# A fused attention and feed-forward kernel: value sums, output products and casts reordered, the last four steps turned by TensorE

## The chip, the cores and the metric

One core of one Trainium2 chip. The metric is the device time of the program in microseconds. Engines: PE is TensorE, DVE is VectorE, ACT is ScalarE, POOL is GpSimd, SP issues the DMAs. Each runs its own program in order and waits for the others at semaphores.

## The reference

Two layers over x of 8 x 128 x 512, each an attention and a feed-forward part with residuals. Nearly all the time goes to the attention of the first layer, with 32 heads of 128:

```python
x = _rmsnorm(hidden_states, ln_weight)
h_q = (x @ w_q.T).reshape(b, lq, H, DH)
h_k = (key_value_states @ w_k.T).reshape(b, lk, H, DH)
h_v = (key_value_states @ w_v.T).reshape(b, lk, H, DH)
score = jnp.einsum('bqhd,bkhd->bhqk', h_q, h_k) + position_bias[None]
score = jnp.where(m, score, -jnp.inf)
score = jnp.where(m, jax.nn.softmax(score, axis=-1), 0.0)
attn = jnp.einsum('bhqk,bkhd->bqhd', score, h_v).reshape(b, lq, H * DH)
return hidden_states + attn @ w_out.T
```

Then come a feed-forward part with low-rank experts, an attention of one head (its product of `wq1` and `wk1` is formed on the chip while the first attention ends), and a feed-forward part with 6-bit weights.

## The kernel before

The attention is cut into 64 steps. A group is two heads, and has four steps of two batches each, so a step holds four 128 x 128 score blocks in one PSUM bank. A turn is eight steps (c = 0 to 7, called step 0 to 7 here); turns 2 to 6 are a hardware loop, the first eight steps, turn 1 and the last turn are written out. The last four steps (60 to 63) also carry the start of the second layer.

Every fp32 operand of a large product is held as a high and a low part (`_hi` in fp32r, made by ACT as a cast; `_lo` by POOL or VectorE as a subtraction), and a product is three matmuls: high by high, high by low, low by high (`three`, lines 363 to 365). Queries and keys of a group are made by seven half-size products each (`q_p1` to `q_p7`, `k_p1` to `k_p7`), the values of two groups by seven products in two halves (`v_p1` to `v_p7`). Each product lands in a PSUM bank (`ps_q`, `ps_q2`, `ps_k`, `ps_k2`, `ps_v`), and VectorE adds it to earlier sums (`q_u2`, `k_c11`, `v_c22`, ...), which frees the bank. The seven weight combinations are formed by POOL and cast by ACT (`high_v1` to `high_v7`, `low_v`, `high_fourth`, `low_third` and so on), one step or more ahead of their use.

A step runs like this. TensorE makes the scores in `ps_s`. VectorE adds mask and bias (`softmax_front`, L1598), takes the row maximum and negates it (`neg_max`, L1602). ACT takes four exponentials with row sums (L787). VectorE forms the factors (reciprocal L1606, `row_fac` L1608) and multiplies (L1611, `softmax_back`). `turn_blocks` transposes 32 x 32 blocks twice, into `probs_t` and in place (L1616, L1617), and ACT copies the twelve off-diagonal blocks to their places (`pt_blocks`, L799). One step later TensorE multiplies by the values (`step_values`, `ps_t`, L2214); ACT casts the result to `att_hi` (`attention_high`, L781), VectorE forms `att_lo` (`attention_rest`, L1476), and TensorE multiplies by the output weights (`output`) in two halves, one batch each, into the single bank `ps_o`. VectorE adds each half into `acc` (`add_output`, L1488); half 1 cannot start until half 0 has been added.

Each engine's order is written out by hand in its own `step(i, c)`: between the parts above stand products, sums, casts and subtractions of coming groups.

## Time and profile before

| | us |
|---|---|
| median of 3 runs (1002.92 to 1004.36) | 1003.94 |
| the profiled execution | 1005.09 |
| its span, first to last instruction | 1003.1 |
| busy: TensorE 93%, VectorE 74%, ACT 60%, POOL 53% of the span | |

A timeline row has its start (from the span's start), its duration, engine, line, operation, the tile written and those read, and in brackets the idle time before it with the instruction that ended it. Matmuls overlap their neighbours, so 128x512 matmuls that take 0.39 us start about 0.23 us apart. The turn shown below starts in step 6: scores of step 7 at 557.45, of step 0 at 569.28, of step 1 at 584.28, of step 3 at 607.92.

### The profile page before, as it was taken

How to read it: one execution, taken by the hardware profiler on the slowest of the kernel's cores; microseconds unless marked ns; L12 is line 12 of the kernel's file. 1: busy time of each engine (PE TensorE's matmuls, PEld its weight loads, DVE VectorE, ACT ScalarE, POOL GpSimd, SP SyncE). 2: the span in 40 equal slices, each digit the busy share in tenths (PEclk: the TensorE clock that was granted, in tenths of full speed). 3: DMA queues.
4: the chain of work that ended last, by engine and by line, in shares of the span. 5: the costliest groups of instructions: out<-in, count | busy, mean ns of one | idle time of the engine just before them, and what ended most of it. 6: DMA issues, size and time to landing. Idle time of an engine off the chain costs nothing.

```text
span 1003.1 us, 17307 instructions
## 1 busy us (share of the span) xinstructions
PE 937.3 (93%) x5261; PEld 796.9 (79%) x5261; DVE 739.3 (74%) x1289; ACT 598.3 (60%) x1847; POOL 527.0 (53%) x582
## 2 busy tenths in 40 slices
PE   9999999999899989998999899989999897889997
PEld 8778888888788878887888778877887776768885
DVE  5676874676787787777787778777877887667787
ACT  5787556465565656665666566656574656344564
POOL 2450636365557656675457555755565643112477
PEclk9999999999999999999999999999999998899999
DMA  9214348644666457645683657364755662130101
GB/s 337 78 65 151 126 153 289 215 167 147 221 223 224 148 213 253 235 146 209 215 269 123 239 184 258 123 248 155 269 166 194 204 216 84 65 116 1 33 22 63
DMA packets 61291, 171.70 MB, mean 171 GB/s; under 512 B 6055, under 2 KB 8491, under 8 KB 60988
## 3 DMA queue, kind: packets, MB, share of 16 engines
q1 hardware_dynamic: 61244, 171.11, 49.6%
q8 instruction: 25, 0.41, 0.2%
q14 instruction: 22, 0.18, 0.1%
HBM read 159.56 MB, written 11.53 MB: 171 GB/s over the span
## 4 chain that ended last, share of the span: by engine, by line
PE 66%; DVE 14%; ACT 8%; issue 8%; POOL 3%; DVEq 1%; DMA 0%; SPq 0%; ACTq 0%; POOLq 0%
PE ps_v L363 5%; PE ps_o L363 5%; PE ps_s L2193 5%; PE ps_o L365 4%; PE ps_o L364 4%; PE ps_v L365 4%; PE ps_v L364 4%; PE ps_q L363 4%; PE ps_q L365 4%; PE ps_q L364 4%; PE ps_k L363 4%; PE ps_k L364 4%; PE ps_k L365 4%; PE ps_t L2214 3%; ACT probs_t L799 3%
## 5 line engine op out<-in xcount | busy, mean ns | idle before, releaser
L799 ACT COPY probs_t<-scores 32x128 f32<-32x128 f32 x768 | 227.6, 296 | 175.8 <-DVE scores L1617 167.6
L787 ACT ACTIVATE scores<-scores,neg_max 128x128 f32<-128x128 f32 x256 | 99.7, 391 | 110.1 <-DVE neg_max L1602 109.7
L1158 POOL TENSOR_TENSOR wq_lo<-raw_q,wq_hi 128x256 fp32r<-128x256 f32 x65 | 57.2, 881 | 150.5 <-ACT wq_hi L620 150.5
L363 PE MATMUL ps_o<-wo_hi,att_hi 128*128 128x512 f32 x256 | 106.4, 416 | 20.0 <-DVE acc L1488 16.2
L1598 DVE TENSOR_TENSOR scores<-ps_s,shift 128x512 f32<-128x512 f32 x64 | 44.2, 691 | 104.4 <-PE ps_s L2193 104.2
L364 PE MATMUL ps_o<-wo_lo,att_hi 128*128 128x512 f32 x256 | 102.4, 400 | 0.0
L365 PE MATMUL ps_o<-wo_hi,att_lo 128*128 128x512 f32 x256 | 102.4, 400 | 0.0
L1488 DVE TENSOR_TENSOR acc<-ps_o,acc 128x512 f32<-128x512 f32 x128 | 86.8, 678 | 17.2 <-PE ps_o L365 17.1
L1476 DVE TENSOR_TENSOR att_lo<-ps_t,att_hi 128x512 fp32r<-128x512 f32 x64 | 44.2, 690 | 65.6 <-ACT att_hi L781 65.6
L1117 POOL TENSOR_TENSOR shift<-bias_sb,mask_sb 128x512 f32<-128x512 f32 x64 | 87.2, 1365 | 1.5 <-DVE scores L1598 1.5
L363 PE MATMUL ps_v<-wv_hi,ct_hi 128*128 128x256 f32 x264 | 78.0, 295 | 6.3 <-DVE vv L1442 2.2
L363 PEld LDWEIGHTS ps_o<-wo_hi,att_hi 128*128 128x128 f32 x256 | 49.2, 192 | 42.7 <-DVE acc L1488 14.9
L1108 POOL TENSOR_TENSOR wo_lo<-raw_o,wo_hi 128x1024 fp32r<-128x1024 f32 x16 | 38.3, 2395 | 75.6 <-ACT wo_hi L717 75.6
L2193 PEld LDWEIGHTS ps_s<-kt,qt 128*128 128x128 f32 x512 | 67.7, 195 | 10.2 <-issue 4.3
L1611 DVE TENSOR_TENSOR scores<-scores,row_fac 128x512 f32<-128x512 f32 x64 | 73.8, 1153 | 2.2
L364 PE MATMUL ps_v<-wv_lo,ct_hi 128*128 128x256 f32 x264 | 75.3, 285 | 0.0
L365 PE MATMUL ps_v<-wv_hi,ct_lo 128*128 128x256 f32 x264 | 75.3, 285 | 0.0
L2193 PE MATMUL ps_s<-kt,qt 128*128 128x128 f32 x512 | 69.1, 278 | 2.4 <-DVE kt L1527 1.5
L363 PE MATMUL ps_v<-wv_hi,ring_hi 128*128 128x256 f32 x144 | 44.1, 306 | 19.9 <-DVE vv L1561 10.7
L363 PE MATMUL ps_q<-xt_hi,wq_hi 128*128 128x512 f32 x148 | 60.9, 411 | 0.0
L363 PEld LDWEIGHTS ps_v<-wv_hi,ct_hi 128*128 128x128 f32 x264 | 50.9, 193 | 10.7 <-issue 3.9
L365 PEld LDWEIGHTS ps_o<-wo_hi,att_lo 128*128 128x128 f32 x256 | 49.3, 193 | 11.1
(394 smaller groups left out, 2850.5 us busy)
## 6 DMA issues: line engine op xcount, KB each, us to landing
ring_hi<-scratch_x_t SPq DMA_DIRECT2D x39, 512.0 KB, 4.0
ring_lo<-scratch_x_t SPq DMA_DIRECT2D x39, 512.0 KB, 4.9
ring_hi<-scratch_c_t SPq DMA_DIRECT2D x39, 512.0 KB, 5.4
ring_lo<-scratch_c_t SPq DMA_DIRECT2D x39, 512.0 KB, 6.2
raw_o<-in_w_o SPq DMA_DIRECT2D x16, 512.0 KB, 3.3
raw_q<-in_w_q SPq DMA_DIRECT2D x15, 512.0 KB, 4.1
raw_k<-in_w_k SPq DMA_DIRECT2D x15, 512.0 KB, 5.2
xt_hi<-scratch_x_t SPq DMA_DIRECT2D x13, 512.0 KB, 5.8
```

Source lines behind the costliest of these rows:

```text
L363: pe.matmul(dst, hi_l, hi_r, start=first, stop=False)
L364: pe.matmul(dst, hi_l, lo_r, start=False, stop=False)
L365: return pe.matmul(dst, lo_l, hi_r, start=False, stop=last)
L787: e = act.activation(probs[n][:, m, :], scores[n][:, m, :], ACT.Exp, bias=neg_max[:, n, m:m + 1], accum_out=row_sum[:, n, m:m + 1])
L799: last = act.copy(block_of(probs_t, j, i), block_of(scores[n], i, j))
L1117: pool.tensor_tensor(shift[n][:].rearrange("p (b h) k -> p b h k", b=2), bias_b, mask_b, ALU.add).then_inc(shift_done, 1)
L1158: pool.tensor_tensor(w_slot(wq_lo, slot), src, w_slot(wq_hi, slot).bitcast(F32), ALU.subtract).then_inc(wq_lo_s, 1)
L1476: dve.tensor_tensor(att_lo[:], blocks(ps_t), att_hi[:].bitcast(F32), ALU.subtract).then_inc(att_lo_s, 1)
L1488: dve.tensor_tensor(acc[:, b, :], ps_o[:], acc[:, b, :], ALU.add).then_inc(o_added, 1)
L1598: dve.tensor_tensor(scores[n][:], blocks(ps_s), shift[n][:], ALU.add).then_inc(s_shifted, 1)
L1611: dve.tensor_tensor(probs[n][:], probs[n][:], row_fac[:, n, :].unsqueeze(2).broadcast_to([P, 4, P]), ALU.mult).then_inc(s_chain, 1)
L2193: last = pe.matmul(ps_s[:, m * P:(m + 1) * P], qt[n][:, h, cols], kt[n][:, h, cols], start=True, stop=True)
```

## The change

What it does, engine by engine.

- VectorE: `softmax_back` is divided. The reciprocal and `row_fac` (`row_factors`) move ahead of `attention_rest`; the multiply joins the two transposes in `turn_blocks`. In step 0 the value sums `v_c22` and `v_u4` move ahead of the multiply, in steps 1 and 2 `v_c12` moves ahead of the output sum, and the output sum of half 0 stands behind the transposes in steps 3 and 7 as in the others. In step 7 `q_c21` moves ahead of `attention_rest`, and `k_u3` behind the output sum.
- TensorE: `output` waits for `att_hi` first, issues the four matmuls that read it, and only then waits for `att_lo`. In step 4 `q_p3` goes ahead of `v_p1`.
- ACT: the value casts `high_v1`, `2`, `5`, `6`, `7` go ahead of the step's exponentials; `attention_high` goes ahead of `q_first`, and `v_first` of half 1 behind `high_sums`.
- POOL: the low value parts go ahead of the weight sums (steps 0, 4), of `low_third` (6) and of `low_fourth` (3, 7).
- The last four steps: VectorE only multiplies (`softmax_back`), TensorE transposes the four blocks into `ps_t` with `ident` (`step_transpose`), and ACT copies the bank to `probs_t` (`pt_evac`). Values are taken in the same step and no longer in the next, and the orders of all engines around them are written anew.

```diff
+WHOLE = STEPS - 4
...
+        def turned(s):
+            return not isinstance(s, int) or s < WHOLE
...
# ACT
+            def pt_evac(s):
+                act.wait_ge(pt_done, s - WHOLE + 1)
+                act.copy(probs_t[:], blocks(ps_t)).then_inc(pt_out, 1)
...
+                if c == 6 and coming:
+                    high_v7(i + 1)
...
                 exponentials(s, n)
                 if c == 4 and coming:
                     v_first(i + 1, 0)
-                    high_v2(i + 1)
+                attention_high(s - 1)
                 if c % 4 == 1 and more:
                     q_first(G)
-                attention_high(s - 1)
...
-            pt_blocks(STEPS - 4, 0, (0, 1, 2, 3))
+            pt_evac(STEPS - 4)
             wk1_high_part(3)
             split_o(GROUPS - 1)
+            attention_high(STEPS - 4)
             exponentials(STEPS - 3, 1)
-            attention_high(STEPS - 4)
...
# POOL
+                if c == 6 and coming:
+                    low_v(i + 1, 4, 0, v_even[0][:])
                 if c % 4 == 2 and more:
                     low_third(G)
...
-                if c == 6 and coming:
-                    low_v(i + 1, 4, 0, v_even[0][:])
...
# VectorE
             def softmax_front(s, n):
                 dve.wait_ge(s_done, s + 1)
                 dve.wait_ge(shift_done, s + 1)
-                wait_from(dve, e_done, s - 1)
-                wait_from(dve, pt_out, 4 * s - 4)
+                wait_from(dve, pt_out, s - 1)
...
+            for c in range(5):
                 step(TURNS - 1, c)
+            add_output(STEPS - 5, 3, (1,))
+            attention_rest(STEPS - 4)
+            softmax_front(STEPS - 3, 1)
+            q_c12(GROUPS - 1)
+            softmax_back(STEPS - 3, 1)
+            add_output(STEPS - 4, 4, (0,))
+            k_c12(GROUPS - 1)
+            wq1_rest(0)
+            wq1_rest(1)
+            add_output(STEPS - 4, 4, (1,))
+            wq1_rest(2)
...
# TensorE
             def output(s, c, g=None, parts=(0, 1)):
-                wait_from(pe, att_lo_s, s + 1)
+                wait_from(pe, att_hi_s, s + 1)
...
                     for h in range(2):
-                        last = three(pe, ps_o[:], att_hi[:, 2 * j + h, :], att_lo[:, 2 * j + h, :],
-                                     wo_hi[:, h, :], wo_lo[:, h, :], h == 0, h == 1)
+                        pe.matmul(ps_o[:], att_hi[:, 2 * j + h, :], wo_hi[:, h, :], start=h == 0, stop=False)
+                        pe.matmul(ps_o[:], att_hi[:, 2 * j + h, :], wo_lo[:, h, :], start=False, stop=False)
+                    if j == 0:
+                        wait_from(pe, att_lo_s, s + 1)
+                    for h in range(2):
+                        last = pe.matmul(ps_o[:], att_lo[:, 2 * j + h, :], wo_hi[:, h, :], start=False, stop=h == 1)
                     last.then_inc(o_done, 1)
...
+            def step_transpose(s, c):
+                pe.wait_ge(p_done, s + 1)
+                wait_from(pe, att_lo_s, s)
+                for m in range(4):
+                    last = pe.transpose(ps_t[:, m * P:(m + 1) * P], probs[c % 2][:, m, :], ident[:])
+                last.then_inc(pt_done, 1)
...
+            s = STEPS - 4
+            wait_projections(g, 4)
+            step_scores(s, 4)
+            q_p5(g)
+            step_values(s - 1, 3, v_count(TURNS - 1, 13))
+            k_p5(g)
+            v_p4(TURNS - 1, 1)
+            output(s - 1, 3, None, (0,))
+            step_transpose(s, 4)
+            output(s - 1, 3, None, (1,))
+            step_values(s, 4, v_count(TURNS - 1, 14))
+
+            s = STEPS - 3
+            wait_projections(g, 5)
+            step_scores(s, 5)
+            q_p3(g)
+            k_p3(g)
+            output(s - 1, 4, g, (0,))
...
+            step_transpose(s, 5)
+            output(s - 1, 4, None, (1,))
+            step_values(s, 5, v_count(TURNS - 1, 14))
...
             step_scores(s, 6)
             product_m(0)
-            step_values(s - 1, 5, v_count(TURNS - 1, 14))
+            output(s - 1, 5, None, (0,))
             product_m(1)
-            output(s - 1, 5, None, (0,))
+            output(s - 1, 5, None, (1,))
+            step_transpose(s, 6)
             product_m(2)
-            output(s - 1, 5, None, (1,))
+            step_values(s, 6, v_count(TURNS - 1, 14))
```

Where the instructions stand now, at three places. First VectorE in step 0 of a loop turn, from `att_lo` or the factors to the output sum. Before (`v_odd_high` and `vv` are the value sums, the first `scores` row is the multiply):

```order
L1476 TENSOR_TENSOR att_lo<-ps_t,att_hi 128x512
L1606 RECIPROCAL row_inv<-row_sum 128x4
L1608 SCALAR_TENSOR_TENSOR row_fac<-row_max,row_inv 128x4
L1611 TENSOR_TENSOR scores_84<-scores_84,row_fac 128x512
L1616 STREAM_TRANSPOSE probs_t<-scores_84 128x512
L1617 STREAM_TRANSPOSE scores_84<-scores_84 128x512
L1561 TENSOR_TENSOR v_odd_high<-ps_v,v_odd_low 128x512
L1561 TENSOR_TENSOR vv_78<-ps_v,vv_78 128x512
L1488 TENSOR_TENSOR acc<-ps_o,acc 128x512
```

Now:

```order
L1618 RECIPROCAL row_inv<-row_sum 128x4
L1620 SCALAR_TENSOR_TENSOR row_fac<-row_max,row_inv 128x4
L1552 TENSOR_TENSOR mid<-ps_q,mid 128x512
L1489 TENSOR_TENSOR att_lo<-ps_t,att_hi 128x512
L1574 TENSOR_TENSOR v_odd_high<-ps_v,v_odd_low 128x512
L1574 TENSOR_TENSOR vv_78<-ps_v,vv_78 128x512
L1625 TENSOR_TENSOR scores_84<-scores_84,row_fac 128x512
L1628 STREAM_TRANSPOSE probs_t<-scores_84 128x512
L1629 STREAM_TRANSPOSE scores_84<-scores_84 128x512
L1501 TENSOR_TENSOR acc<-ps_o,acc 128x512
```

The factors stand ahead of `att_lo`, and the two value sums stand ahead of the multiply and the transposes.

Second, VectorE in step 7 of a loop turn, up to the end of the turn (`acc` is the output sum of half 0, the last `kt` row the key sum that the next scores read). Before:

```order
L1476 TENSOR_TENSOR att_lo<-ps_t,att_hi 128x512
L1506 TENSOR_TENSOR kt_74<-ps_k,kt_74 128x512
L1606 RECIPROCAL row_inv<-row_sum 128x4
L1608 SCALAR_TENSOR_TENSOR row_fac<-row_max,row_inv 128x4
L1611 TENSOR_TENSOR scores_86<-scores_86,row_fac 128x512
L1488 TENSOR_TENSOR acc<-ps_o,acc 128x512
L1517 TENSOR_TENSOR kt_77<-ps_k,mid 128x512
L1522 TENSOR_TENSOR qt_73<-ps_q,qt_76 128x512
L1527 TENSOR_TENSOR kt_74<-ps_k,kt_77 128x512
L1616 STREAM_TRANSPOSE probs_t<-scores_86 128x512
L1617 STREAM_TRANSPOSE scores_86<-scores_86 128x512
```

Now:

```order
L1618 RECIPROCAL row_inv<-row_sum 128x4
L1620 SCALAR_TENSOR_TENSOR row_fac<-row_max,row_inv 128x4
L1535 TENSOR_TENSOR qt_73<-ps_q,qt_76 128x512
L1489 TENSOR_TENSOR att_lo<-ps_t,att_hi 128x512
L1519 TENSOR_TENSOR kt_74<-ps_k,kt_74 128x512
L1625 TENSOR_TENSOR scores_86<-scores_86,row_fac 128x512
L1628 STREAM_TRANSPOSE probs_t<-scores_86 128x512
L1629 STREAM_TRANSPOSE scores_86<-scores_86 128x512
L1501 TENSOR_TENSOR acc<-ps_o,acc 128x512
L1530 TENSOR_TENSOR kt_77<-ps_k,mid 128x512
L1540 TENSOR_TENSOR kt_74<-ps_k,kt_77 128x512
```

The output sum stands behind both transposes, and the key sum stands last, one sum nearer to the output sum.

Third, ACT in the last turn, from the exponentials of step 60 to the casts of `wq1`. Before:

```order
L787 ACTIVATE scores_84,row_sum<-scores_84,neg_max 128x128 x4
L781 CAST att_hi<-ps_t 128x512
L908 CAST wk_hi<-wk_raw 128x512 x3
L799 COPY probs_t<-scores_84 32x4x32 x12
L908 CAST wk_hi<-wk_raw 128x512
L717 CAST wo_hi<-raw_o 128x1024
L787 ACTIVATE scores_86,row_sum<-scores_86,neg_max 128x128 x4
L781 CAST att_hi<-ps_t 128x512
L922 CAST wq_hi<-wq_low 128x512 x2
L799 COPY probs_t<-scores_86 32x4x32 x12
L922 CAST wq_hi<-wq_high_158 128x512
```

Now:

```order
L795 ACTIVATE scores_84,row_sum<-scores_84,neg_max 128x128 x4
L789 CAST att_hi<-ps_t 128x512
L921 CAST wk_hi<-wk_raw 128x512 x3
L812 COPY probs_t<-ps_t 128x512
L921 CAST wk_hi<-wk_raw 128x512
L725 CAST wo_hi<-raw_o 128x1024
L789 CAST att_hi<-ps_t 128x512
L795 ACTIVATE scores_86,row_sum<-scores_86,neg_max 128x128 x4
L935 CAST wq_hi<-wq_low 128x512 x2
L812 COPY probs_t<-ps_t 128x512
L935 CAST wq_hi<-wq_high_158 128x512
```

One copy of a PSUM bank stands for the twelve block copies, and `att_hi` stands ahead of the exponentials of the next step.

## Rows read from the trace of the kernel before

**Rows 1.** Windows: length, busy us of the engines, PEclk, DMA share, GB/s.
```profile
447.70:552.58 104.88, 99.14 (x561) 84.68 (x560) 79.30 (x132) 63.30 (x211) 62.18 (x66) 0.98 0.60 203
552.58:656.05 103.47, 97.59 (x562) 83.45 (x560) 79.45 (x132) 63.29 (x211) 62.28 (x66) 1.00 0.59 205
827.50:885.40 57.90, 44.65 (x208) 36.11 (x206) 38.90 (x63) 28.43 (x89) 10.79 (x7) 0.87 0.29 98
```

**Rows 2.** Table of waits, TensorE: line, releaser, us in total, times, longest.
```profile
PE ps_o L363 <- DVE acc L1488: 16.2, 15, 3.3
PE ps_v L363 <- DVE vv L1561: 12.2, 11, 2.0
PE ps_v L363 <- POOL wv_lo L1204: 9.2, 6, 1.6
...
PE ps_o L363 <- DVE att_lo L1476: 2.8, 3, 2.2
```

**Rows 3.** Timeline of one turn, TensorE, steps 6, 7, 0, 0, 1, 3.
```profile
554.53 0.38 PE L363 MATMUL ps_v<-wv_hi,ring_hi 128*128 128x256 f32 x1 [1.56 <-POOL wv_lo L1204]
...
567.30 0.50 PE L363 MATMUL ps_o<-wo_hi,att_hi 128*128 128x512 f32 x1 [0.58 <-DVE acc L1488]
...
569.28 0.37 PE L2193 MATMUL ps_s<-kt,qt 128*128 128x128 f32 x1 [0.31 <-DVE kt L1527]
...
581.36 0.39 PE L363 MATMUL ps_v<-wv_hi,ring_hi 128*128 128x256 f32 x1 [1.73 <-DVE vv L1561]
...
589.27 0.39 PE L363 MATMUL ps_v<-wv_hi,ct_hi 128*128 128x256 f32 x1 [0.31 <-DVE vv L1561]
...
618.40 0.50 PE L363 MATMUL ps_o<-wo_hi,att_hi 128*128 128x512 f32 x1 [1.19 <-DVE acc L1488]
```

**Rows 4.** Timeline, POOL, step 7 (value part) and step 1 (output weights).
```profile
564.81 1.29 POOL L1204 TENSOR_TENSOR wv_lo<-raw_v_odd,wv_hi 128x512 fp32r<-128x512 f32 x1
...
585.61 2.40 POOL L1108 TENSOR_TENSOR wo_lo<-raw_o,wo_hi 128x1024 fp32r<-128x1024 f32 x1 [4.85 <-ACT wo_hi L717]
```

**Rows 5.** Timeline, VectorE, step 0 of the same turn.
```profile
576.66 0.69 DVE L1476 TENSOR_TENSOR att_lo<-ps_t,att_hi 128x512 fp32r<-128x512 f32 x1 [1.66 <-ACT att_hi L781]
...
577.67 1.12 DVE L1611 TENSOR_TENSOR scores<-scores,row_fac 128x512 f32<-128x512 f32 x1
...
580.63 0.67 DVE L1561 TENSOR_TENSOR vv<-ps_v,vv 128x512 f32<-128x512 f32 x1
```

**Rows 6.** Timeline, VectorE, step 7 and (last row) step 3.
```profile
564.44 0.43 DVE L1608 SCALAR_TENSOR_TENSOR row_fac<-row_max,row_inv 128x4 f32<-128x4 f32 x1
564.90 1.75 DVE L1611 TENSOR_TENSOR scores<-scores,row_fac 128x512 f32<-128x512 f32 x1
...
568.96 0.69 DVE L1616 STREAM_TRANSPOSE probs_t<-scores 128x512 f32<-128x512 f32 x1
...
614.72 1.25 DVE L1608 SCALAR_TENSOR_TENSOR row_fac<-row_max,row_inv 128x4 f32<-128x4 f32 x1
```

**Rows 7.** Timeline, ACT, step 60: block copies, and a cast of `att_hi`.
```profile
838.61 3.67 ACT L799 COPY probs_t<-scores 32x128 f32<-32x128 f32 x12 [3.48 <-DVE scores L1617]
...
847.95 0.56 ACT L781 CAST att_hi<-ps_t 128x512 fp32r<-128x512 f32 x1
```

**Rows 8.** Groups of instructions, TensorE: a later stage's transposes.
```profile
L2646 PE MATMUL ps_s<-ident,normed 128*128 128x128 f32 x32 | 4.8, 272 | 0.0
```

**Rows 9.** Timeline, TensorE, last four steps: the four longest waits.
```profile
839.30 0.58 PE L363 MATMUL ps_o<-wo_hi,att_hi 128*128 128x512 f32 x1 [3.29 <-DVE acc L1488]
...
849.29 0.50 PE L363 MATMUL ps_o<-wo_hi,att_hi 128*128 128x512 f32 x1 [2.20 <-DVE att_lo L1476]
...
871.46 1.87 PE L2589 MATMUL ps_v<-ones,w_rows 128*128 128x1 f32 x8 [3.54 <-DVE w_rows L1835]
...
884.28 2.07 PE L2573 MATMUL ps_q<-w_rows,ones 128*128 128x512 f32 x2 [3.69 <-DVE mm_lo L1840]
```

**Rows 10.** Timeline, VectorE, step 1: `neg_max`.
```profile
586.92 1.11 DVE L1602 TENSOR_SCALAR neg_max<-row_max 128x4 f32<-128x4 f32 x1
```

More of the change, by code:

```diff
@@ L357, in v_weight, with chain @@
             return 7 * p - 10 + n
+        def turned(s):
+            return not isinstance(s, int) or s < WHOLE
+        def chain(s, n):
+            return 5 * s + n if turned(s) else 5 * WHOLE + 3 * (s - WHOLE) + n
         block = stack.enter_context(nc.Block())
@@ L789, in exponentials, with pt_blocks @@
                 e.then_inc(e_done, 1)
-            def pt_blocks(s, n, rows):
+            def pt_blocks(s, n):
                 act.wait_ge(p_done, s + 1)
-                for i in rows:
+                for i in range(4):
                     for j in range(4):
@@ L868, in step @@
                     high_sums(G)
+                if c == 4 and coming:
+                    v_first(i + 1, 1)
                 if c % 4 == 1 and more:
@@ L1269, in step @@
                 coming = not last
+                if c == 0 and own:
+                    low_v(i, 6, 0, v_even[1][:])
+                if c == 4 and coming:
+                    low_v(i + 1, 2, 0, v_even[1][:])
                 if c % 4 == 0 and more:
@@ L1305, in step @@
                     low_v(i, 7, 0, v_odd[1][:])
-                if c == 6 and coming:
-                    low_v(i + 1, 4, 0, v_even[0][:])
-                if c % 4 == 3 and more:
-                    low_fourth(G)
                 if c == 3 and coming:
@@ L1313, in step @@
                     low_v(i + 1, 5, 1, v_odd[0][:])
+                if c % 4 == 3 and more:
+                    low_fourth(G)
             for s in range(FIRST):
@@ L1731, in step @@
                         v_evac(12, 2, 0, done=15)
-                if c == 3 and own:
-                    v_c21(i, 0)
-                if last and c == 5:
-                    q_c12(g)
+                if turned(s):
+                    row_factors(s, n)
+                if c % 4 == 0 and summed:
+                    q_u4(g)
+                if c % 4 == 1 and summed and not (last and c == 5):
+                    k_c12(g)
+                if c == 6 and coming:
+                    v_u2(i + 1, 1)
+                if c == 3:
+                    k_u3(G)
+                    if own:
+                        v_c21(i, 0)
+                if c == 7:
+                    q_c21(G)
                 attention_rest(s - 1)
+                if c == 3:
+                    q_c21(G)
                 if c == 7:
                     k_c11(G)
-                if c == 3:
-                    q_c21(G)
-                softmax_back(s, n)
-                if c % 4 == 3:
-                    add_output(s - 1, (c - 1) % LOOP_STEPS, (0,))
-                    if c == 7:
-                        k_u3(G)
-                        q_c21(G)
-                    k_c21(G)
-                turn_blocks(s, n)
                 if c == 0 and own:
@@ L1752, in step @@
                     v_u4(i, 0)
-                if c == 5 and coming:
-                    v_c11(i + 1, 1)
-                if c % 4 != 3:
-                    add_output(s - 1, (c - 1) % LOOP_STEPS, (0,))
+                if turned(s):
+                    turn_blocks(s, n)
+                else:
+                    softmax_back(s, n)
                 if c == 1:
@@ L1761, in step @@
                         v_evac(14, 3, 0, done=13)
+                if c == 2 and own:
+                    v_c12(i, 1)
+                if c == 5 and coming:
+                    v_c11(i + 1, 1)
+                add_output(s - 1, (c - 1) % LOOP_STEPS, (0,))
+                if c == 7:
+                    k_u3(G)
+                if c % 4 == 3:
+                    k_c21(G)
                 if c % 4 == 2:
                     q_c11(G)
-                if c == 2 and own:
-                    v_c12(i, 1)
                 if last and c == 4:
@@ L1774, in step @@
                     block_low(1, wide[0], 7)
-                if last and c == 5:
-                    k_c12(g)
-                    for m in range(3):
-                        wq1_rest(m)
             def target_experts():
@@ L2435, in step @@
                     q_p6(G)
-                if last and c == 5:
-                    q_p3(g)
                 if c == 6:
@@ L2514, in step @@
                     k_p4(G)
-                if last and c == 5:
-                    pe.wait_ge(v_out, v_count(i, 14))
-                    for _ in range(4):
-                        pe.matmul(ps_v[:, 0:P], ones[:], ones[:], start=True, stop=True)
                 output(s - 1, (c - 1) % LOOP_STEPS, None, (1,))
@@ L2527, in _ @@
                     step(i, c)
-            for c in range(6):
+            for c in range(4):
                 step(TURNS - 1, c)
+            g = GROUPS - 1
+            s = STEPS - 4
[12 more added lines that the diff above has]
+            step_scores(s, 5)
+            q_p3(g)
+            k_p3(g)
+            output(s - 1, 4, g, (0,))
+            pe.wait_ge(v_out, v_count(TURNS - 1, 14))
+            for _ in range(4):
+                pe.matmul(ps_v[:, 0:P], ones[:], ones[:], start=True, stop=True)
+            step_transpose(s, 5)
+            output(s - 1, 4, None, (1,))
+            step_values(s, 5, v_count(TURNS - 1, 14))
             def product_m(m):
```

102 lines of the change are left out of this document (42 added, 60 removed).

## The prediction

> **What bounds the kernel now.** I read the table of waits of TensorE first, then the windows, then the timelines of one loop turn and of the last four steps. In a whole turn of the loop TensorE is busy 97.59 of 103.47 us, and no other engine is above 80 [rows 1]. So the time is TensorE's work plus TensorE's waits, and a change that adds next to no matmuls can save only waits. The table of waits names them: 16.2 us for the output sum `acc`, 12.2 for the value sums `vv` (L1561), 9.2 for the low value weights of POOL, 2.8 for `att_lo` [rows 2]. They come in two places. In a turn the same waits return: 1.56 us for `wv_lo` in step 6, 0.58 for `acc` and 0.31 for `kt` around step 7, 1.73 for `vv` in step 0, 0.31 in step 1, 1.19 for `acc` in step 3 [rows 3]. The last four steps hold the largest: a stretch of 57.90 us in which TensorE is busy only 44.65, at a granted clock of 0.87 [rows 1].
>
> The profiled execution took 1005.09 us around a span of 1003.1; the median shown is 1003.94, so 1.15 comes off at the end.
>
> **The change, part by part.**
>
> Step 6, low value weights first. `v_p7` waits for the fifth low value part; on ACT its cast stood behind the exponentials and the casts of `high_third`, on POOL behind four more subtractions. Now the cast goes while ACT would wait for `neg_max`, and POOL's part (1.29 us, [rows 4]) goes ahead of those four. It is there some five us early, so the 1.56 us go, in six turns the 9.2 us of [rows 2]. What is late next is the output sum of half 0, which ends hardly before TensorE would want it; I take **-9.0**. The weight loads on SP's queue that wait for POOL's parts start no later: the query and key parts that the value part is moved past begin only when their own casts arrive.
>
> Step 0, value sums ahead of the passes. Before, `att_lo` (0.69) was followed by the factors, the multiply (1.12), two transposes, and only then by the two sums; the last started at 580.63 [rows 5]. In the new order the two sums follow `att_lo` at once: 576.66 + 0.69 + 2 x 0.64 = 578.6, a us before TensorE wants them, so the 1.73 us go. But the multiply, both transposes and the output sum then end near 581.8, and TensorE, no longer held up, wants half 1 at about 581.1 (581.36 - 1.73, and some 1.5 for the value product before it). So 0.7 us come back; -1.0 in six turns is **-6.0**.
>
> Steps 7 and 3, output sum behind both transposes. Before, it stood between the multiply and the transposes. It now has to wait for two transposes of 0.69 more [rows 6], some 1.35 us, less the two small factor instructions, which move into VectorE's wait for `att_hi`: with the reciprocal's 0.17 about 0.6 us in step 7, and 1.4 in step 3, where the factor instruction took 1.25 [rows 6]. In step 7 that is +0.75 on the 0.58 us wait, while the 0.31 for `kt` goes because the key sum now stands third behind the multiply and no longer fourth: +0.45 in six turns, **+2.6**. In step 3 it cancels: **0**. This is the least certain term, since the multiply takes 1.75 us where it meets POOL and 1.12 in step 0 [rows 5, 6]: if step 7 finds POOL idle it gains 1 us a turn instead.
>
> `att_lo` waited for late. Four of six output matmuls need only `att_hi`, some 0.9 us of cover. In the turns it covers 0.1 us in steps 3 and 7, and the `acc` wait that follows absorbs it: **0**. Ahead of the loop some 0.6 us of `att_lo` and part of POOL's weights (which come earlier as the factors run inside a wait) give **-1.0**.
>
> TensorE's clock. The turn of 104.88 us had a mean granted clock of 0.98, the one of 103.47 a clock of 1.00 [rows 1]: 1.41 us for a spell at the lower of its two levels, behind the 1.73 us wait, in every second turn. If that wait goes the spell may go, but step 7 now waits 1.3 us or more. I take half of 2.5 spells: **-1.8**.
>
> The last four steps. ACT no longer turns blocks by twelve copies, 3.67 us, but copies one bank, about 0.56 us like the cast of `att_hi` [rows 7]; VectorE drops eight transposes of 0.7; TensorE gains sixteen transposes, 0.6 us for each four by the row of the later stage's transposes [rows 8], three fours of them in this stretch: +1.8. The four waits are 3.29 for `acc`, 2.20 for `att_lo`, 3.54 for `w_rows` and 3.69 for `mm_lo` [rows 9], 12.7 in all. The first goes because add_output no longer stands behind transposes and collided factors, the second because `att_hi` comes before the exponentials on ACT, the third and fourth because values of a step are done in that step, so that nothing of it is left between `w_rows`, the fourth product and `mm_lo`. The clock: 13% of 57.90 us is 7.5 us, some of it during idle time; I take 5. New waits: the first transposes wait for the multiply (about 1.5 us), the second 0.6, the product with `wq1` about 1.3 for VectorE's low parts, the `w_rows` product 0.6; 4 in all. -12.7 - 5 + 1.8 + 4 = **-12** (bounds -6, if the serial chain of scores, exponentials, multiply, turn and values costs 2 us more in three steps, and -16).
>
> Behind this stretch the chain is TensorE's own work and moves with it.
>
> **Sum.** -9.0 - 6.0 + 2.6 - 1.0 - 1.8 - 12 = -27.2. The profiled execution would take 1005.1 - 27.2 = 977.9, the median 1.15 less: **977 us**.
>
> **Rivals.**
>
> A. Everything clears: no remainder in step 0 (-10.5), step 7 meets no POOL (-6), all clock spells go (-3.5), tail -12 with the rest: -9 - 10.5 - 6 - 1 - 3.5 - 12 = -42, **962 us**. For it: the places are independent and each needs only tenths. Against it: the same two transposes stand ahead of the output sum in every step.
>
> B. The order alone takes the gain back. Half 1 has little room: if the output sum is 0.85 us later in every loop step, steps 0, 1, 3 and 7 show it whole and step 2 half, about 3.9 us a turn. Six turns are 23 us, the loop's gain is 22, and only the tail's 12 stay: **992 us**. Against it: the factors' lead offsets half of the two transposes.
>
> C. The moved casts meet `neg_max`. The row shows it: `neg_max`, four numbers a lane, took 1.11 us and ended with POOL's 2.40 us subtraction of the output weights [rows 4, 10]. The new order sends POOL's value part (1.29 us, [rows 4]) off shortly before `neg_max` in steps 0, 3, 4 and 7, and may bring the 2.40 us subtraction onto it in step 1. If 0.7 us of it reaches the output sum in four steps of six turns, 17 us of the gain go: **994 us**. The Trainium skill has this as a rule (SBUF — State Buffer, Who interferes with whom): whichever of VectorE and GpSimd issues first holds their shared port pair for its whole instruction, and the other fully blocks; by that rule it is the start, to a tenth of a us, that decides, and the trace agrees with 1.11 us in place of a few tenths.
>
> D. Slower: VectorE's output sum bounds every step. If the factors do not get their lead, because the exponentials end late behind the casts, it is 1.4 us late. Less the room at half 1 (estimates from the turn of [rows 3]: none in steps 0, 1, 3, 7, about 0.4, 1.8, 1.0, 0.7 in 2, 4, 5, 6) that is 7.6 us a turn, 46 in six, against 34 gained: **1016 us**. It decides from about 1.1 us of lateness. Against it: the exponentials wait for `neg_max` in most steps, so a cast ahead of them costs nothing.
>
> **How the numbers follow.** Forecast 0.48, A 0.18, B 0.12, C 0.10, D 0.08, an outcome that cancels within 2 us 0.04. The forecast's own range is 968 to 986. To leave out 2 in 10, the range reaches to A below and to B above: 960 to 992. About 0.2% is what a measurement of this kernel can tell from no change. Faster 0.88, same 0.04, slower 0.08.
>
> **What would show it.** In the profile after: no wait for `wv_lo` in step 6; none above 1 us for `vv`; waits for `acc` in steps 7 and 3 that stay or grow, to 1 to 2 us; the stretch from the scores of step 60 to the first product with `mm_hi` at about 46 us instead of 57.9; granted clock there above 0.9. The forecast is wrong if `acc` waits grow beyond 30 us in all, if new waits for `probs_t` appear in the last four steps, or if `neg_max` is long in most steps.

## The result, and the profile after

The changed kernel takes 960.14 us (959.27 to 961.76, 4 runs) where the one before took 1003.43 (1001.01 to 1004.36, 4 runs): 43.3 us less, a ratio of 0.957 (interval 0.955 to 0.960). The forecast was 977, so its direction held and its size was short by 17 us; the time lies at the very end of the range (960 to 992), near rival A's 962.

| profiled execution | before | after |
|---|---|---|
| span, us | 1003.1 | 958.3 |
| mean granted clock | 0.985 | 0.996 |
| TensorE busy | 93% | 96% |
| a turn of the loop, us | 103.5 or 104.9 | 99.3, all five |
| scores of step 60 to the first product with `mm_hi`, us | 57.9 | 42.4 |

The windows of the changed kernel (start and end, length, busy us of TensorE, its weight loads, VectorE, ACT and POOL, granted clock, DMA share, GB/s): a turn of the loop, from the scores of its first step to those of the next turn, and the stretch of the last four steps.

```profile
552.79:652.10 99.31, 96.14 (x561) 83.76 (x561) 77.37 (x130) 64.47 (x212) 63.07 (x65) 1.00 0.62 213
799.94:842.36 42.42, 41.70 (x226) 34.88 (x224) 31.69 (x57) 17.59 (x49) 11.24 (x7) 0.96 0.30 98
```

They answer to [rows 1]. In the last steps TensorE is now busy 41.7 of 42.4 us; before it was 44.65 of 57.9. The table of waits of TensorE in the changed kernel (what waited and for whom, us in total, times, longest):

```profile
PE ps_o L2200 <- DVE acc L1501: 21.2, 16, 3.0
PE ps_k L371 <- POOL wk_lo L1112: 2.4, 2, 1.6
PE ps_v L371 <- DVE v_odd_low L1574: 2.4, 5, 0.5
```

Of [rows 2], `wv_lo` in the turns and `vv` (L1561, now L1574) are gone; `acc` grew from 16.2 to 21.2; `v_odd_low` is new, five times 0.49. The same rows in the timeline of TensorE for one turn, steps 7, 0, 3 and 4, and then the start of the products with `mm_hi` (start, length, and in brackets the idle time and who ended it):

```profile
551.21 0.50 PE L2200 MATMUL ps_o<-wo_hi,att_hi 128*128 128x512 f32 x1 [1.06 <-DVE acc L1501]
...
564.64 0.50 PE L2200 MATMUL ps_o<-wo_hi,att_hi 128*128 128x512 f32 x1
...
599.48 0.50 PE L2200 MATMUL ps_o<-wo_hi,att_hi 128*128 128x512 f32 x1 [1.54 <-DVE acc L1501]
...
605.25 0.39 PE L371 MATMUL ps_v<-wv_hi,ct_hi 128*128 128x256 f32 x1 [0.49 <-DVE v_odd_low L1574]
...
842.36 0.80 PE L371 MATMUL ps_q<-ct_hi,mm_hi 128*128 128x512 f32 x1
```

Against [rows 3]: 0.58 became 1.06 in step 7, the 1.73 for the value sums of step 0 is gone and half 1 there waits 0.08 for `acc` (no bracket: under what is listed), 1.19 became 1.54 in step 3, and the 0.49 in step 4 had not been there. Where the time went shows best in the distances of the scores of successive steps, of which I take one turn without a clock spell on either side (before 569.28 to 672.74, after 552.79 to 652.10):

| step | 0 | 1 | 2 | 3 | 4 | 5 | 6 | 7 | turn |
|---|---|---|---|---|---|---|---|---|---|
| before, us | 15.00 | 12.22 | 11.42 | 11.99 | 14.61 | 13.06 | 13.33 | 11.83 | 103.46 |
| after, us | 13.34 | 11.46 | 11.42 | 11.97 | 15.10 | 13.01 | 11.52 | 11.49 | 99.31 |

Step 6 gains 1.81, step 0 1.66, step 1 0.76, step 7 0.34; step 4 loses 0.49.

### The profile page after: what moved, and what is told of

Its sections match the earlier page's. It is cut to its first block, busy times and chain, and to the rows that moved or that the text cites. A ratio compares the mean times of both kernels' runs of the same rounds, so it can differ in the third digit from the quotient of the medians.

```text
span 958.3 us, 17189 instructions
## 1 busy us (share of the span) xinstructions
PE 917.9 (96%) x5277; PEld 791.3 (83%) x5277; DVE 717.1 (75%) x1281; ACT 593.7 (62%) x1803; POOL 533.6 (56%) x582
## 4 chain that ended last, share of the span: by engine, by line
PE 79%; DVE 11%; issue 4%; ACT 3%; POOL 1%; DMA 1%; DVEq 0%; SPq 0%; ACTq 0%; POOLq 0%
PE ps_o L2200 6%; PE ps_s L2221 6%; PE ps_q L371 6%; PE ps_q L373 6%; PE ps_q L372 6%; PE ps_o L2205 5%; PE ps_o L2201 5%; PE ps_v L371 5%; PE ps_k L371 5%; PE ps_t L2249 5%; PE ps_k L372 5%; PE ps_v L373 5%; PE ps_v L372 5%; PE ps_k L373 5%; DVE scores L1625 2%
## 5 line engine op out<-in xcount | busy, mean ns | idle before, releaser
L807 ACT COPY probs_t<-scores 32x128 f32<-32x128 f32 x720 | 213.4, 296 | 116.5 <-DVE scores L1629 108.6
L2200 PE MATMUL ps_o<-wo_hi,att_hi 128*128 128x512 f32 x256 | 102.7, 401 | 23.1 <-DVE acc L1501 21.2
L1171 POOL TENSOR_TENSOR wq_lo<-raw_q,wq_hi 128x256 fp32r<-128x256 f32 x65 | 48.2, 741 | 98.6 <-ACT wq_hi L628 98.6
L2205 PE MATMUL ps_o<-wo_hi,att_lo 128*128 128x512 f32 x256 | 79.9, 394 | 0.0
L1217 POOL TENSOR_TENSOR wv_lo<-raw_v_even,wv_hi 128x512 fp32r<-128x512 f32 x24 | 31.0, 1291 | 84.9 <-ACT wv_hi L681 84.9
L1625 DVE TENSOR_TENSOR scores<-scores,row_fac 128x512 f32<-128x512 f32 x60 | 59.4, 990 | 0.0
L373 PE MATMUL ps_q<-xt_hi,wq_lo 128*128 128x512 f32 x148 | 57.8, 391 | 0.0
L372 PE MATMUL ps_q<-xt_lo,wq_hi 128*128 128x512 f32 x148 | 57.8, 391 | 0.0
```

The lines of the kernel that those rows point to most:

```text
L372: pe.matmul(dst, hi_l, lo_r, start=False, stop=False)
L373: return pe.matmul(dst, lo_l, hi_r, start=False, stop=last)
L807: last = act.copy(block_of(probs_t, j, i), block_of(scores[n], i, j))
L1625: dve.tensor_tensor(probs[n][:], probs[n][:], row_fac[:, n, :].unsqueeze(2).broadcast_to([P, 4, P]), ALU.mult).then_inc(s_chain, 1)
L2200: pe.matmul(ps_o[:], att_hi[:, 2 * j + h, :], wo_hi[:, h, :], start=h == 0, stop=False)
L2205: last = pe.matmul(ps_o[:], att_lo[:, 2 * j + h, :], wo_hi[:, h, :], start=False, stop=h == 1)
```

## The experiments

Twelve kernels. E1 keeps little but the last four steps; E2 to E4, E8, E9 and E12 undo one part of the change each; E5 to E7, E10 and E11 go on from it. What undoing costs is told against the changed kernel's 960.1 us.

**E1, the last four steps alone.** The places of the casts, VectorE's order in the turns and the early wait for `att_lo` are as before. TensorE's order in the turns is still that of the change: `q_p3` ahead of `v_p1` in step 4 and, not in the list of the change above, the key product `k_p1` ahead of `v_p3` in step 1. The led factors of the first eight steps stay too.

> The last four steps as in the change, all else (the casts' places, VectorE's order in the turns, att_lo waited for early) as before. Theory P, the parts add up: between the scores of step 60 and the end the changed kernel is 17.3 us shorter than before (499.332 + ... in the two traces: the scores of step 60 lie 27.57 us earlier, the last matmul 44.84 us), so 1003.4 - 17.3 = 986 us, with the turns at 103.5 and 104.9 us as before. Theory Q, the parts lean on each other: the last steps need the late wait for att_lo and a turn that leaves no backlog, so less than the 12 us of the prediction are left: 992 us or more.

986.8 us (ratio to before 0.985, 0.982 to 0.988). From the scores of step 60 to the last matmul it takes 154.9 us, 171.8 before and 154.6 in the changed kernel: the last steps' gain stands by itself, theory P. (The 499.332 in the expectation is a slip for 999.33, the end of the last matmul before.) But its turns are not those of before: step 4 is 0.26 us shorter and step 5 1 us longer in every turn, though VectorE, ACT and POOL have their old orders there. VectorE and POOL in step 5, first before, then in E1:

```profile
635.90 2.39 POOL L1108 TENSOR_TENSOR wo_lo<-raw_o,wo_hi 128x1024 fp32r<-128x1024 f32 x1 [0.32 <-ACT wo_hi L717]
...
637.15 1.17 DVE L1602 TENSOR_SCALAR neg_max<-row_max 128x4 f32<-128x4 f32 x1
```

```profile
635.92 2.37 POOL L1120 TENSOR_TENSOR wo_lo<-raw_o,wo_hi 128x1024 fp32r<-128x1024 f32 x1
...
636.10 2.21 DVE L1613 TENSOR_SCALAR neg_max<-row_max 128x4 f32<-128x4 f32 x1
```

`neg_max`, four numbers a lane, is 2.21 us long in E1, 1.17 before, and 0.17 where POOL is idle. In both kernels it ends with POOL's 2.4 us subtraction of the output weights, at the same 638.3 us. Counted from the scores of step 0, `neg_max` starts 0.49 us earlier in E1 than before (67.39 for 67.88) and POOL's subtraction 0.59 later (67.21 for 66.62); so VectorE waits a us longer for POOL, and TensorE gets a wait of 0.72 us for the value sum behind it. TensorE's order in steps 1 and 4 is what is left as a cause of the shift, but no run undoes it alone.

**E2, casts and low value weights in their old places** (on ACT `attention_high` and `v_first` too; the cut shows one step of ACT).

```diff
-                if c == 7 and coming: high_v5(i + 1)      # ACT, and c 0, 3, 4, 5, 6 alike
                 exponentials(s, n)
...
+                if c == 7 and coming: high_v5(i + 1)
                 pt_blocks(s, n)
```

> The change with ACT's casts and POOL's low value weights in the places they had before. Theory P: in six turns step 6 gets its 1.82 us back (+10.9), and step 4 loses the new 0.49 us wait for v_odd_low (-2.9): 960.1 + 8 = 968 us. Theory Q: the moved weights also kept POOL off the multiply of step 7, which took 1.75 us before and 1.16 after; with it back the output sum there is 0.6 us or more later in six turns, and row factors late behind the casts add some tenths in others: 972 us or more, and a multiply of 1.6 to 1.8 us in step 7.

968.5 us (0.968, 0.966 to 0.970): theory P's time, +8.3, though not by its two terms alone. `wv_lo` is waited for six times again, 10.3 us; the wait of step 7 stays at 1.05 and the multiply at 1.16, so theory Q falls. The 0.49 of step 4 goes, but a wait for `vv` of 0.73 comes in step 5: `neg_max` meets the 2.4 us subtraction there for 2.23 us, as in E1. The loop is 2.1 us a turn longer, and turn 1 is 2.4 shorter.

**E3, VectorE's order in the turns as before.** Value sums behind the passes, output sum ahead of the transposes in steps 3 and 7, factors right ahead of the multiply.

> The change with VectorE's order in the turns as before (value sums behind the passes, output sum ahead of the transposes in steps 3 and 7, factors not led). Theory P: steps 0 and 1 get 2.42 us a turn back (+14.5), the clock its spell of 1.41 us in every second turn (+3.5), step 7 some tenths: 978 to 980 us, with a wait for the value sums of about 1.7 us in step 0. Theory Q, only the value sums' 1.7 us matter and the old place of the output sum is the better one in steps 3 and 7: +10 - 7 = 963 us or less.

985.9 us (0.987, 0.984 to 0.990): +25.8, more than either theory gave. Against E1, which differs by the moved casts and the late `att_lo`, it is 0.9 us faster, although the 9.2 us for `wv_lo` are gone from its waits. Two timeline rows of TensorE, steps 0 and 4, show where they went:

```profile
580.14 0.39 PE L371 MATMUL ps_v<-wv_hi,ring_hi 128*128 128x256 f32 x1 [2.36 <-DVE vv L1574]
...
629.80 0.39 PE L371 MATMUL ps_v<-wv_hi,ct_hi 128*128 128x256 f32 x1 [1.49 <-ACT vv L676]
```

The wait for the value sums in step 0 is 2.36 us now, more than the 1.73 of [rows 3], and step 4 has a new one of 1.49 for ACT's copy of a value part, which the change put behind the casts of the weight sums. So the casts bring 8.3 us with VectorE's new order and about nothing without it: undone singly the three parts cost 8.3, 25.8 and 1.0 us, undone together (E1) 26.7.

**E4, `att_lo` waited for early.**

> The change with the wait for att_lo ahead of all six output matmuls, as before. Theory P: in the turns att_lo is there in time or an acc wait absorbs it, so 960 to 961.5 us (some tenths in the last four steps). Theory Q: with the factors ahead of it on VectorE att_lo comes later than before, so that the wait would show in several steps: 0.3 us in three steps of six turns, 966 us.

961.2 us (0.961, 0.958 to 0.963): theory P, and the 1.0 us lies within what the runs differ by. It waits for `att_lo` 6.1 us in all, and for `acc` 11.5 in place of 21.2: the one takes the place of the other.

**E5, the output sum ahead of the transposes again** (shortened to words).

```diff
+                if c in (3, 7): multiply; add_output(s - 1, ..., (0,)); key sums; transposes
-                multiply; transposes; add_output(s - 1, ..., (0,)); key sums
```

> The change, but in steps 3 and 7 the output sum of half 0 and the key sums stand ahead of the two transposes again (the rest as in the change). Theory P: the changed kernel's waits for acc, 1.06 us in step 7 and 1.54 in step 3 of each turn, are the two transposes' doing and go but for some 0.2 us: 2.3 us in each of some six turns, 946 to 949 us. Theory Q: the transposes now end later, ACT's block copies and the cast and exponentials behind them too, and the output sum of the next step is late by as much as was gained: 956 us or more, with new waits for acc in steps 0 and 4.

953.9 us (0.952, 0.948 to 0.956): 6.2 faster than the change, between the theories. In a turn of the loop steps 3 and 7 are 1.3 us shorter each, as P had it, but 2.0 of the 2.6 us come back, 0.97 in step 0 (a wait for `acc` of 1.05) and 1.0 in step 4; over the five turns 2.9 us are gained, and turn 1 is 2.4 shorter. What step 4 waits for, ACT, POOL and TensorE in one timeline:

```profile
600.44 1.28 POOL L1217 TENSOR_TENSOR wv_lo<-raw_v_even,wv_hi 128x512 fp32r<-128x512 f32 x1 [7.40 <-ACT wv_hi L681]
...
605.87 0.72 POOL L1185 TENSOR_TENSOR w_sum<-raw_k 128x256 f32<-128x256 f32 x1
...
606.62 0.41 ACT L632 CAST wk_hi<-w_sum 128x256 fp32r<-128x256 f32 x1 [2.17 <-POOL w_sum L1185]
...
606.93 0.58 ACT L676 COPY vv<-ps_v 128x512 f32<-128x512 f32 x1
...
607.57 0.39 PE L371 MATMUL ps_v<-wv_hi,ct_hi 128*128 128x256 f32 x1 [1.50 <-ACT vv L676]
```

ACT's copy of the value part stands behind the cast of a weight sum that POOL had not made: POOL had waited 7.40 us for its value part, which its queue holds ahead of the sums.

**E6, POOL's low value weights in step 4 behind `low_first`.** And **E7**, the same on top of E5.

> The change, but in step 4 POOL's low value weights come behind the weight sums and low_first. Theory P: neg_max of step 4 (1.10 us in the changed kernel, 0.17 where it meets no POOL instruction) is long because it meets the 1.29 us subtraction of the low value weights; moved, it is 0.17 again and the 0.49 us wait for v_odd_low in step 4 goes in six turns: 957 us. Theory Q: POOL's work only shifts, and what stands there instead meets VectorE in its place (neg_max of step 4 or 5 over 1 us): 960 us within 1.

> The edits of the two runs before together. Theory P: the two places are independent and the gains add: 943 to 946 us. Theory Q: with TensorE 2 us a turn earlier VectorE's neg_max meets other instructions of POOL (rest_o in step 1, make_shift), or POOL's chain through step 4 bounds it, and half or less of the sum is left: 951 us or more.

965.9 us (0.964, 0.961 to 0.967) and 955.9 us (0.954, 0.951 to 0.957): E6 is 5.7 us slower than the change, E7 2.0 slower than E5, little against the 3.6 by which its own runs differ. In E6 `neg_max` of step 4 is 0.17 again and the 0.49 us gone, as P had it, but the low weights are now waited for, 1.43 us in each turn of the loop; both theories missed it, since they ask when the part is made, not when it is used. E5 had neither the long `neg_max` nor the 0.49, so in E7 there was nothing to win; the low weights are waited for 1.81 us where E5 waits 1.50 for ACT. Its time is theory Q's, which had named POOL's chain through step 4 as one of two causes.

**E8, factors right ahead of the multiply.**

```diff
-                if turned(s): row_factors(s, n)           # while VectorE would wait for att_hi
...
+                if turned(s): row_factors(s, n)
                 if turned(s): turn_blocks(s, n)
```

> The change, but the reciprocal and the factor stand right ahead of the multiply (VectorE's order else as in the change). Theory P, the prediction's: the lead takes two small instructions, 0.35 us or more where they meet POOL, out of the chain to the output sum; steps 3 and 7 show it whole and step 0 partly: 0.7 to 1.2 us a turn, 965 to 968 us. Theory Q: the small instructions only fill time in which VectorE waits for att_hi anyway or, behind it, cost as much as they did ahead; 960 to 962 us.

982.0 us (0.979, 0.976 to 0.983): +21.8 for two small instructions a step, far over both theories. Step 7 shows how. VectorE, and POOL beside it, in the changed kernel, then in E8 with TensorE's wait:

```profile
545.92 0.17 DVE L1620 SCALAR_TENSOR_TENSOR row_fac<-row_max,row_inv 128x4 f32<-128x4 f32 x1
...
547.95 0.74 POOL L1176 TENSOR_TENSOR wk_lo<-raw_k,wk_hi 128x256 fp32r<-128x256 f32 x1
...
548.08 1.16 DVE L1625 TENSOR_TENSOR scores<-scores,row_fac 128x512 f32<-128x512 f32 x1
...
548.65 1.74 POOL L1130 TENSOR_TENSOR shift<-bias_sb,mask_sb 128x512 f32<-128x512 f32 x1
...
550.50 0.65 DVE L1501 TENSOR_TENSOR acc<-ps_o,acc 128x512 f32<-128x512 f32 x1
```

```profile
562.53 0.43 DVE L1620 SCALAR_TENSOR_TENSOR row_fac<-row_max,row_inv 128x4 f32<-128x4 f32 x1
...
562.90 1.29 POOL L1130 TENSOR_TENSOR shift<-bias_sb,mask_sb 128x512 f32<-128x512 f32 x1
...
563.00 1.74 DVE L1625 TENSOR_TENSOR scores<-scores,row_fac 128x512 f32<-128x512 f32 x1
...
566.00 0.65 DVE L1501 TENSOR_TENSOR acc<-ps_o,acc 128x512 f32<-128x512 f32 x1
...
566.71 0.50 PE L2199 MATMUL ps_o<-wo_hi,att_hi 128*128 128x512 f32 x1 [2.30 <-DVE acc L1501]
```

Led, the factors take 0.17 each; unled, the second takes 0.43 beside POOL, and the multiply then starts 0.10 us behind POOL's `make_shift` and takes 1.74 in place of 1.16. The wait for `acc` is 2.30, not 1.06. It is so in every step: without the lead all eight multiplies of a turn start 0.09 to 0.17 us behind an instruction of POOL, and over the 64 steps the multiplies take 78.8 us, where the change has 62.2. Steps 0, 1, 2 and 3 lose too, 1.0, 0.3, 0.3 and 1.1 us a turn. Part of this is TensorE's clock: the granted clock of the turns is 0.97 or 0.98, with six spells at the lower level in the five turns, where the change has none. At the 1.41 us of the turns before this is an estimated 8 of the 20 us by which the five turns are longer.

**E9, the last four steps in the new order, but turned in 32x32 blocks.**

> The change, but the last four steps are turned as all others are, by VectorE's transposes and ACT's twelve copies, in the new order of the work. Theory P, the turning by TensorE carries the gain: on the way from the multiply to the values two transposes (1.4 us) and the copies (3.7) stand where sixteen-fold less stood (0.6 for TensorE's four, 0.6 for one copy), 3.9 us more in each step; in three steps of the stretch little of it is covered: 968 to 972 us. Theory Q, the order carries it (output sum ahead of the low weights, att_hi ahead of the exponentials, values in their own step): 962 us or less.

967.0 us (0.966, 0.962 to 0.969): +6.8, near P. Of the 17.3 us in the last steps some 7 are the turning's, some 10 the order's (the turning undone in the new order; the old order with TensorE's turning was not run). Step 60 in E9 (ACT's copies, TensorE's wait), and the same place in the changed kernel (TensorE's four transposes, ACT's one copy):

```profile
807.86 3.67 ACT L807 COPY probs_t<-scores 32x128 f32<-32x128 f32 x12 [2.26 <-DVE scores L1628]
...
811.58 1.16 PE L2242 MATMUL ps_t<-probs_t,v_odd_low 128*128 128x128 f32 x8 [1.41 <-ACT probs_t L807]
```

```profile
808.71 0.60 PE L2238 MATMUL ps_t<-ident,scores 128*128 128x128 f32 x4
...
809.34 0.59 ACT L812 COPY probs_t<-ps_t 128x512 f32<-128x512 f32 x1 [1.52 <-PE ps_t L2238]
```

From the multiply to the values there are 0.60 us of transposes and 0.59 of a copy where E9 has two transposes of VectorE, 1.4, and 3.67 of copies. The Trainium skill (VectorE: DVE Perf Modes, Rules for kernel authors) advises TensorE for a 128x128 transpose whose result may lie in PSUM; the trace agrees in these steps, where the turning is on the chain.

**E10, E5 with POOL's low value weights between the weight sums and `low_first`;** **E11, on top of it the value casts of steps 0 and 4 behind the exponentials and `att_hi`.**

```diff
                     weight_sums(G, 1, raw_k, wk_in)       # POOL; in E11 for c == 0 too
+                if c == 4 and coming: low_v(i + 1, 2, 0, v_even[1][:])
                 if c % 4 == 0 and more: low_first(G)
...
                 exponentials(s, n)                        # ACT, E11
                 attention_high(s - 1)
+                if c == 0 and own: high_v3(i)
+                if c == 4 and coming: high_v2(i + 1)
```

> Run e5 (output sum first in steps 3 and 7), and in step 4 POOL's low value weights behind the weight sums but ahead of low_first. Theory P: the 1.50 us wait of e5 in step 4, for ACT's first value part, comes from POOL's weight sums, which start only behind the low value weights (6.5 us of waiting on POOL); with the sums ahead the wait goes in six turns: 953.9 - 9 = 945 us. Theory Q: as in e7 another wait takes its place (wv_lo over 1 us, or neg_max meeting POOL in step 4): 951 us or more.

> Run e10, and in steps 0 and 4 the value cast on ACT behind the exponentials and the cast of att_hi, POOL's value part in step 0 behind the weight sums too. Theory P: in those steps, in the order with the output sum first, the block copies end late, so that a cast ahead of the exponentials delays them by 0.5 us and the output sum with them (1.05 us wait in step 0 of e5); moved, 0.5 us a turn goes on top of e10: 942 us. Theory Q: the late low value weights are waited for instead, and it is e10 or worse.

943.5 us (0.942, 0.939 to 0.946) and 939.5 us (0.939, 0.935 to 0.942): theory P twice, and E11 is 20.6 us faster than the change. Its waits of TensorE:

```profile
PE ps_o L2214 <- DVE acc L1501: 6.5, 15, 1.7
PE ps_k L371 <- POOL wk_lo L1112: 2.4, 2, 1.6
```

The 9.0 us for ACT's value part of E5 are gone with E10, and `acc` fell from 21.2 in the change to 11.8 in E10 and 6.5 in E11. E11's two moves, ACT's casts and POOL's part in step 0, were not tried apart.

**E12, the value sums behind the passes again,** all else as in the change.

> The change, but in step 0 the two value sums stand behind the multiply and the transposes again, the output sum behind them as before. Theory P, the prediction's reading: the sums' place is what the 1.73 us wait of step 0 hung on, but the factors' lead has shortened VectorE's chain meanwhile: from the changed kernel's trace the multiply would start at 560.3 in place of 561.7, the second sum end near 564.0, and TensorE, which now asks at 563.0, would wait 1.0 us; the output sum behind them is in time then, so 1.0 us a turn and no clock spell: 966 us. Theory Q: the whole wait is back, 1.7 us in each of some six turns, and with it the stretches at the lower clock level: 970 us or more.

968.1 us (0.965, 0.963 to 0.968): +8.0, between the theories and nearer P. A turn takes 100.59 us, 1.28 more: 0.64 in step 0 (a wait of 0.72 for the sums) and 0.66 in step 1, where the output sum is late in its turn and is waited for 0.39 us. POOL and VectorE in step 1, in E12, then in the changed kernel:

```profile
571.19 2.40 POOL L1121 TENSOR_TENSOR wo_lo<-raw_o,wo_hi 128x1024 fp32r<-128x1024 f32 x1 [4.14 <-ACT wo_hi L725]
...
572.40 1.21 DVE L1614 TENSOR_SCALAR neg_max<-row_max 128x4 f32<-128x4 f32 x1
```

```profile
568.67 0.17 DVE L1614 TENSOR_SCALAR neg_max<-row_max 128x4 f32<-128x4 f32 x1
...
568.88 2.39 POOL L1121 TENSOR_TENSOR wo_lo<-raw_o,wo_hi 128x1024 fp32r<-128x1024 f32 x1 [4.91 <-ACT wo_hi L725]
```

With the sums late `neg_max` meets POOL's subtraction again, as before the change; with the sums early it is done just ahead of it. The granted clock is 1.00 in all five turns.

## Why the prediction was right in sign and too small

All terms, from the distances of the scores in the two profiled executions (span -44.8 us):

| term | predicted | measured |
|---|---|---|
| step 6, low value weights | -9.0 | -10.8 |
| step 0, value sums (with step 1) | -6.0 | -14.8 |
| step 7 | +2.6 | -2.0 |
| step 3 | 0 | -0.1; +3.4 in turn 1 and the last |
| first steps, and step 1 of turn 1 | -1.0 | -1.8 |
| TensorE's clock (three spells in the loop) | -1.8 | -4.2 |
| the last four steps | -12 | -17.3 |
| step 4 | none | +3.1 |
| steps 2 and 5 | none | -0.3 |

**Step 6** was right in mechanism and size (E2).

**Step 0** is where the prediction failed most: "So 0.7 us come back; -1.0 in six turns". That the wait for the value sums goes is right, but nothing came back: TensorE waits 0.08 us for half 1. The 581.8 of the prediction is 578.6 and the multiply, two transposes and the output sum at their old lengths (1.12, 2 x 0.69, 0.67), 12.5 us behind the scores of the step. The output sum ended at 11.8. `att_lo` came 0.57 us earlier than before (6.81 us behind the scores, 7.38 before), so that the second value sum ended at 9.0 and not at 9.3; and the multiply, 0.95, and the three instructions behind it, which start some 0.6 us apart, took 2.8 us and not 3.2. This room hangs on the factors' lead: without it (E8) the sum ends at 12.5 and half 1 waits 0.76, the prediction's remainder. When the output sum of half 0 ends, counted from the scores of its step, and how long the multiply takes, in one turn (before from 569.28, the change from 552.79, E8 from 568.29):

| step | 0 | 1 | 2 | 3 | 4 | 5 | 6 | 7 |
|---|---|---|---|---|---|---|---|---|
| sum ends, before, us | 12.62 | 10.67 | 9.68 | 10.42 | 11.41 | 10.68 | 9.68 | 9.80 |
| the change | 11.80 | 9.71 | 9.68 | 10.42 | 11.90 | 10.63 | 9.68 | 9.86 |
| E8 | 12.49 | 10.16 | 10.22 | 10.71 | 12.14 | 10.64 | 9.68 | 11.11 |
| multiply, before, us | 1.12 | 1.19 | 1.20 | 1.74 | 0.70 | 0.69 | 1.20 | 1.75 |
| the change | 0.95 | 0.68 | 1.03 | 1.38 | 1.12 | 0.70 | 1.00 | 1.16 |
| E8 | 1.20 | 1.20 | 1.20 | 1.74 | 1.19 | 1.12 | 1.20 | 1.74 |

The prediction gave the lead a price only in steps 7 and 3, as a set-off against the transposes, and only by the factors' own length. E8 puts it at 22 us, its clock spells included, more than the 8 of the sums' own place (E12).

**Step 1** gained 0.76 a turn that was not in the sum. `neg_max` no longer meets POOL's subtraction there (0.17 for the 1.11 of [rows 10]), and that hangs on the value sums: with them late (E12) it takes 1.21 again and 0.66 of the 0.76 come back. The margin is narrow: POOL's subtraction starts 0.21 us behind `neg_max`. The key product that TensorE now does ahead of the value product that waited 0.31 does not bring it alone: E1 and E3 have it, and step 1 takes 12.21 us, 12.22 before.

**Steps 7 and 3.** TensorE's wait for the output sum grew by 0.48 and 0.35, but the sum itself is hardly later: it ends 0.06 us later in step 7 and at the same time in step 3 (table). TensorE comes to it earlier. In step 7 the mis-sized piece is the +0.75: the prediction left the multiply at the 1.75 of [rows 6], and it took 1.16. The wait for `kt` went, as predicted; by the starts of the matmuls (half 1 to the next scores, 1.98 us before, 1.57 after) that is 0.41. Hence -0.34 a turn where +0.45 stood. In step 3 the 0 held in the loop; in turn 1 and in the last turn the step is 2.1 and 1.3 us longer, and E5, with the sum ahead of the transposes, takes this back. That two transposes ahead of the sum cost 1.3 us in both steps is what E5 shows.

**Clock.** Half of the spells were taken; all three of the loop's went.

**The last four steps.** The four old waits went, as predicted. The mis-sized piece is "New waits", "4 in all": TensorE shows 0.44 us for `acc` and 0.25 for `wq_lo` in this stretch, and none for the transposes, since the output matmuls of half 0 ahead of them cover the multiply. (In E6 and E12, with the same last steps, the first multiply takes 1.73 us in place of 0.69 and the first transposes wait 1.1, but from the scores of step 60 to the end these take no longer.) That accounts for 3.3 of the 5.3 us; another 1.8 lie behind the stretch (112.1 us from the first product with `mm_hi` to the end, 114.0 before), where the prediction let the chain only move along.

That the time lies inside the range at all is luck: step 3 of turn 1 and of the last turn (+3.4) and step 4 (+3.1), which the prediction did not have, took back 6.5 us, without which the kernel would have been near 954. Of the signs that the prediction named, the waits for `acc` in steps 7 and 3 stayed, and the stretch's granted clock was 0.96; none of the three that would have refuted it came: `acc` 21.2 us in all, no wait for `probs_t` in the last four steps, `neg_max` over 1 us in 16 of the 64 steps.

**Rival C** came true in part, with a price in one step of a turn: `neg_max` of step 4 (POOL and VectorE, the changed kernel).

```profile
603.29 1.29 POOL L1217 TENSOR_TENSOR wv_lo<-raw_v_even,wv_hi 128x512 fp32r<-128x512 f32 x1 [6.33 <-ACT wv_hi L681]
...
603.51 1.10 DVE L1614 TENSOR_SCALAR neg_max<-row_max 128x4 f32<-128x4 f32 x1
...
604.52 0.68 DVE L1574 TENSOR_TENSOR v_odd_low<-ps_v,v_odd_low 128x512 f32<-128x512 f32 x1
```

POOL's value part starts 0.22 us ahead of `neg_max`, which ends with it; TensorE pays 0.49 us a turn. By the Trainium skill (SBUF — State Buffer, Who interferes with whom) whichever of the two starts first holds their shared port pair for its whole instruction; the trace agrees here, with 1.10 us for 0.17. Summed over all steps, the time by which `neg_max` is over 0.17 us hardly changed, 23.2 us before and 21.5 after: the collisions moved, mostly from steps 1 and 6 to steps 0 and 4. **Rival B**, the order alone, did not come: the output sum ends earlier in steps 0 and 1 and as before in steps 2, 3 and 6 (table). **Rival D**, no lead, is what E8 tries: the kernel loses half of its gain, but at 982 us is still faster than before. The 1016 were too much because the sum is not 1.4 us late in every step: against the change it is 0.2 to 0.7 late in steps 0 to 4, 1.25 in step 7 and not at all in 5 and 6. **Rival A** had the time nearly right, by terms that were not: it had too much in step 7 (-6), too little in steps 0 and 1, 6 and the last steps, and none of the losses in steps 3 and 4.

## What to carry to other kernels

Where one engine's chain decides, move out of it whatever can run while that engine would wait, however short: two small instructions led by a few us brought 22 us here, since the long pass behind them meets less of POOL's work, and TensorE's clock stays up. Judge an order by the engine that consumes it: the moved casts gained about nothing with VectorE's old order, and 8 us with the new one. And when a step of a queue is moved, look up when its result is used, not only when it can be made (E6, E7).

## What the runs showed of the hardware

An engine can lose a us a turn with its order unchanged, because it reaches a place earlier and another engine reaches it later (E1: VectorE and POOL have their old orders in the turns, and `neg_max` of step 5 takes 2.21 us for 1.17). In the fourteen traces each of the 382 `neg_max` (of 896) that took 0.2 us or more had started while an instruction of POOL was under way; the others take 0.17 to 0.19 us, 134 of them in the last 0.16 us of such an instruction, but for one that started together with it. The collision works in the other direction too: POOL's `make_shift` takes 1.29 us where it starts ahead of the multiply (step 7 of E8), and 1.74 where the multiply had started 0.57 ahead of it (step 7 of the change).

When TensorE's clock falls is not settled by the length of one wait: in five turns of the loop the granted clock of a turn was 0.98 or below (of 2.4 GHz; within a spell the matmuls go at 1.2) in three with waits of 1.73 us in step 0, in two of E3 with 2.36, in one of E1 with 1.74, in all five of E8 with waits of 2.30 and 1.83 elsewhere, and in none of the change with 1.06 and 1.54. What decides between these stays open.
